# First attention of a four-stage network: transposes and value weighing one step later behind the scores, a third buffer for the first map, output weights in the raw weights' buffer

## The reference, cut to what matters

```python
qkv = hidden_states @ Wqkv_w.T + Wqkv_b
p1 = attn_map(q[:, :, :, 0], k[:, :, :, 0])      # causal softmax(q k / sqrt(128))
p2 = attn_map(q[:, :, :, 1], k[:, :, :, 1])
p = p1 - lam * p2
o = einsum('bhqk,bhke->bqhe', p, v)
o = o * rsqrt(mean(o * o) + EPS) * subln_w * (1 - LAMBDA_INIT)
return o.reshape(B, S, H * D) @ out_w.T + out_b
```

## Time and profile before

| | us |
|---|---|
| median of 3 runs | 1652.39 |
| the three runs | 1649.94 to 1653.19 |
| profiled execution | 1637.22 |
| its span | 1635.4 |

### The profile page before, as it was taken

The page is one execution under the profiler, slowest core; times in us unless marked ns, Lnnn a source line. Parts: engine busy times, 40 slices in busy tenths (PEclk is TensorE's granted clock), DMA queues, the critical chain, the costliest instruction groups (busy, mean ns, idle before and its releaser), DMA issues.

```text
span 1635.4 us, 30982 instructions
## 1 busy us (share of the span) xinstructions
PE 1526.0 (93%) x10518; PEld 1317.8 (81%) x10518; DVE 1105.6 (68%) x2963; ACT 938.1 (57%) x2054; POOL 637.2 (39%) x578
## 2 busy tenths in 40 slices
PE   8899999999999999999998999899999999998996
PEld 7888888888888677688987888888888886776885
DVE  7667767677745787574687676676767377884756
ACT  5666565665544577653656556556655346775453
POOL 2635444654561100243545445444654510031642
PEclk9999999999999999999999999999999999999998
DMA  3110000020120432124310100000202113322233
GB/s 133 46 53 17 27 1 16 26 90 3 40 70 10 71 56 52 30 108 142 110 73 14 65 17 27 17 4 22 92 1 57 52 32 63 59 65 81 68 133 111
DMA packets 48202, 88.08 MB, mean 54 GB/s; under 512 B 9600, under 2 KB 30480, under 8 KB 46928
## 3 DMA queue, kind: packets, MB, share of 16 engines
q1 hardware_dynamic: 43552, 75.28, 16.1%
q0 software_dynamic: 3744, 10.26, 1.8%
q10 hardware_dynamic: 768, 0.79, 0.2%
HBM read 60.18 MB, written 19.76 MB: 49 GB/s over the span
## 4 chain that ended last, share of the span: by engine, by line
PE 62%; DVE 15%; ACT 10%; issue 8%; POOL 4%; ACTq 1%; DMA 1%; DVEq 0%; POOLq 0%; SPq 0%
PE ps L410 15%; PE ps L412 14%; PE ps L411 14%; PE ps L1193 4%; PE ps L1210 4%; PE ps L1153 4%; ACT E L1407 4%; DVE E L1816 2%; PE ps L916 2%; POOL E L2286 2%; ACT PT_h L1389 1%; DVE On L1724 1%; PE ps L1189 1%; PE ps L846 1%; POOL xs L2397 1%
## 5 line engine op out<-in xcount | busy, mean ns | idle before, releaser
L1407 ACT ACTIVATE E<-E,nmax 128x128 f32<-128x128 f32 (+7 forms) x256 | 197.3, 772 | 211.6 <-DVE nmax L1816 211.1
L2283 POOL TENSOR_SCALAR E<-E,mixc 128x128 f32<-128x128 f32 (+7 forms) x128 | 97.6, 762 | 400.9 <-DVE mixc L1782 400.9
L1568 ACT ACTIVATE PT<-ps 128x512 f32<-128x512 f32 x288 | 154.9, 600 | 58.7 <-PE ps L1193 57.7
L2286 POOL TENSOR_TENSOR E<-E 128x128 f32<-128x128 f32 (+7 forms) x128 | 182.8, 1428 | 10.7
L410 PE MATMUL ps<-V_h,PT_h 128*128 128x256 f32 x576 | 164.7, 286 | 1.7 <-DVE O L1794 1.7
L412 PE MATMUL ps<-V_h,PT_l 128*128 128x256 f32 x576 | 162.7, 283 | 0.0
L411 PE MATMUL ps<-V_l,PT_h 128*128 128x256 f32 x576 | 162.7, 282 | 0.0
L410 PE MATMUL ps<-K_h,Q_h 128*128 128x512 f32 (+3 forms) x384 | 142.7, 372 | 6.3 <-DVE nmax L1816 2.9
L1789 DVE TENSOR_TENSOR PT_l<-ps,PT_h 128x128 fp32r<-128x128 f32 (+7 forms) x128 | 96.7, 755 | 63.2 <-ACT PT_h L1389 62.6
L2036 DVE CUSTOM_DVE_ANT_0 masked<-ps,causal 128x128 bf16<-128x128 f32 (+3 forms) x256 | 110.9, 487 | 39.7 <-PE ps L1153 38.0
L411 PE MATMUL ps<-K_l,Q_h 128*128 128x512 f32 (+3 forms) x384 | 133.8, 348 | 0.0
(11 more groups left out here) (267 smaller groups left out, 4579.1 us busy)
## 6 DMA issues: line engine op xcount, KB each, us to landing
Wa_raw<-in_wa SPq DMA_DIRECT2D x8, 1024.0 KB, 6.0
Fw_raw<-in_fa SPq DMA_DIRECT2D x32, 256.0 KB, 2.7
E_raw<-in_fe SPq DMA_DIRECT2D x8, 768.0 KB, 7.5
xs<-in_xs SPq DMA_DIRECT2D x2, 2967.0 KB, 12.0
Wo_raw<-in_wo SPq DMA_DIRECT2D x8, 512.0 KB, 3.6
yg<-ys SPq DMA_DIRECT2D x8, 512.0 KB, 5.7
xg<-xs SPq DMA_DIRECT2D x6, 645.0 KB, 7.8
KS<-QK_h SPq DMA_DIRECT2D x56, 64.0 KB
```

The costliest lines, as they stand in the source:

```text
L1407: nc.scalar.activation(e[:, 0:w], e[:, 0:w], ACT.Exp, scale=-1.0, bias=nmax[:, s % 4, m:m + 1], accum_out=lsum[:, s % 4, m:m + 1]).then_in ...
L1568: nc.scalar.activation(PT[:, at:at + HALF], bank1(RING1 + n % RING1), ACT.Exp, scale=SCALE1).then_inc(t_used, 1)
L2283: nc.gpsimd.tensor_scalar(e2, e2, mixc[:, n % 4:n % 4 + 1], 1.0, ALU.mult, ALU.mult).then_inc(mix_scaled, 1)
L2286: nc.gpsimd.tensor_tensor(e1, e1, e2, ALU.add).then_inc(p_ready, 1)
```

## The change

- The transposes of a map are issued three steps behind its scores, not two (`TURN_LAG`), and with them `high` and `low`. The weighing and `output` are issued four steps behind, not three (`WEIGH_LAG`); `squares` start at step 5, not 4.
- `E1` has three buffers, `E2` still two. VectorE's second maximum of step s, from step 2 on, also waits for `p_ready` of step s - 2.
- The tail begins with one more transpose ("t" 13) and one more weighing ("v" 12); in the groups with units the tokens are dealt out anew.
- `Wo_raw` is no buffer of its own; it is the first half of `Wa_raw`. So the load of the output weights waits until the next group's `Wa_raw` has been split (step 11), and the load of `Wa_raw` waits until the output weights of the group before have been subtracted (`wo_lo`).

```diff
+E1_RING = 3
+TURN_LAG, WEIGH_LAG = 3, 4
...
-        E1 = [sb(f"E1_{i}", [P, T], F32, s) for i in range(2)]
+        E1 = [sb(f"E1_{i}", [P, T], F32, s) for i in range(E1_RING)]
...
-        Wo_raw = sb("Wo_raw", [P, 4, HID], F32, s)
+        Wo_raw = Wa_raw[:, 0].rearrange("p (c n) -> p c n", n=HID)
...
         if last:
-            return [("t", STEPS0 - 2), ("r", 0), ("v", STEPS0 - 3), ("n", 0), ("n", 1), ("t", STEPS0 - 1), ("o", 0),
-                    ("v", STEPS0 - 2), ("o", 1), ("v", STEPS0 - 1)]
-        return [("t", STEPS0 - 2), *u[0:2], ("v", STEPS0 - 3), *u[2:4], ("t", STEPS0 - 1), ("v", STEPS0 - 2), ("r", 0),
-                *u[4:9], ("v", STEPS0 - 1), *u[9:10], ("r", 1), *u[10:]]
+            return [("t", STEPS0 - 3), ("v", STEPS0 - 4), ("t", STEPS0 - 2), ("r", 0), ("v", STEPS0 - 3), ("n", 0), ("n", 1),
+                    ("t", STEPS0 - 1), ("o", 0), ("v", STEPS0 - 2), ("o", 1), ("v", STEPS0 - 1)]
+        return [("t", STEPS0 - 3), *u[0:2], ("v", STEPS0 - 4), *u[2:4], ("t", STEPS0 - 2), ("v", STEPS0 - 3), ("r", 0),
+                *u[4:6], ("t", STEPS0 - 1), ("v", STEPS0 - 2), *u[6:9], ("v", STEPS0 - 1), *u[9:10], ("r", 1), *u[10:]]
...
         def next_wa(b, g):
             sp.wait_ge(wa_lo, 4 * (b * GROUPS0 + g) + 4)
+            sp.nop(nofuse=True)
+            sp.wait_ge(wo_lo, b * GROUPS0 + g + 1)
+            sp.nop(nofuse=True)
             load_wa(g + 1)
+
+        def load_wo(b, g):
+            sp.wait_ge(wa_lo, 4 * (b * GROUPS0 + g) + 8)
+            sp.nop(nofuse=True)
+            sp.dma_start(Wo_raw, d["wo0"][g]).then_inc(wo_in, 16)
...
             sp.wait_ge(pj_dve, it * UNITS_IT + UNITS_IT)
             sp.nop(nofuse=True)
-            sp.wait_ge(wo_lo, it + 1)
-            sp.dma_start(Wo_raw[:], d["wo0"][g]).then_inc(wo_in, 16)
             load_ba(g + 1)
...
+            load_wo(b, 0)
+            if b == 0:
                 sp.wait_ge(w2_ready, 4)
...
                 group_loads(b, g)
+                load_wo(b, g)
...
             for s in range(STEPS0):
-                if s >= 2:
-                    transpose_p(s - 2)
+                if s >= TURN_LAG:
+                    transpose_p(s - TURN_LAG)
...
-                if s >= 3:
-                    weigh_values(s - 3)
+                if s >= WEIGH_LAG:
+                    weigh_values(s - WEIGH_LAG)
...
-                if s >= 2:
-                    high(s - 2)
+                if s >= TURN_LAG:
+                    high(s - TURN_LAG)
...
-                if s >= 4:
-                    squares(s - 4)
+                if s > WEIGH_LAG:
+                    squares(s - WEIGH_LAG - 1)
...
-                if s >= 2:
-                    low(s - 2)
+                if s >= TURN_LAG:
+                    low(s - TURN_LAG)
...
-                for m, e in ((0, E1[s % 2]), (1, E2[s % 2])):
+                for m, e in ((0, E1[s % E1_RING]), (1, E2[s % 2])):
+                    if m == 1 and s >= 2:
+                        dve.wait_ge(p_ready, STEPS0 * it + s - 1)
                     dve.wait_ge(s_ready[m], STEPS0 * it + s + 1)
```

More of the change, by code:

```diff
@@ L915, in transpose_p @@
                 for kb in range(q_tile(n, last) + 1):
-                    mm = nc.tensor.transpose(ps[2][:, tile(kb)], E1[n % 2][:, tile(kb)], ident[:])
+                    mm = nc.tensor.transpose(ps[2][:, tile(kb)], E1[n % E1_RING][:, tile(kb)], ident[:])
                 mm.then_inc(pt_ps, 1)
             for s in range(STEPS0):
-                if s >= 2:
-                    transpose_p(s - 2)
+                if s >= TURN_LAG:
+                    transpose_p(s - TURN_LAG)
                 if s == 0:
@@ L1442, in attn0_group @@
                         act.wait_ge(wo_scaled, KC * it + KC)
[L1443 removed]
+                        nc.scalar.copy(Wo_h[:], Wo_raw).then_inc(wo_hi, 1)
                     squares(n - 1)
@@ L1806, in attn0_group @@
                     out_normalise(it - 1, g + 1, s - 2)
-                if s >= 2:
-                    low(s - 2)
+                if s >= TURN_LAG:
+                    low(s - TURN_LAG)
                 if s == NT:
                     project_out(s, 0)
-                    output(s - 3)
-                for m, e in ((0, E1[s % 2]), (1, E2[s % 2])):
+                    output(s - WEIGH_LAG)
+                for m, e in ((0, E1[s % E1_RING]), (1, E2[s % 2])):
+                    if m == 1 and s >= 2:
+                        dve.wait_ge(p_ready, STEPS0 * it + s - 1)
                     dve.wait_ge(s_ready[m], STEPS0 * it + s + 1)
@@ L2279, in attn0_group @@
                 w = (q_tile(n, last) + 1) * P
-                e1, e2 = E1[n % 2][:, 0:w], E2[n % 2][:, 0:w]
+                e1, e2 = E1[n % E1_RING][:, 0:w], E2[n % 2][:, 0:w]
                 pool.wait_ge(mix_ready, STEPS0 * it + n + 1)
@@ L2297, in attn0_group @@
             pool.wait_ge(wo_hi, it + 1)
-            low(Wo_l[:], Wo_raw[:], Wo_h[:]).then_inc(wo_lo, 1)
+            low(Wo_l[:], Wo_raw, Wo_h[:]).then_inc(wo_lo, 1)
         def ffn_split(b, c):
```

2 lines of the change are left out of this document (1 added, 1 removed).

## The result

The changed kernel took 1664.5 us (median of 4 runs, 1664.2 to 1667.6), the kernel before, timed beside it, 1652.3 (4 runs, 1649.9 to 1653.2). Ratio 1.0080, 95% interval 1.0063 to 1.0098: 12 to 13 us slower. The forecast was 1660, 7.6 over before, in a range of 1644 to 1668.

The account below looks back on a forecast made before the run. A gapless ring of ScalarE and VectorE bounds most steps, TensorE a middle group's steps 10 to 12 and its end. Middle +2.5, first -3.9, last groups +9.0 make +7.6 us; on the timed median 1652.4 that gives 1660, range 1644 to 1668.

Parts of the forecast that it names:

- Ring: Steps 2 to 9 of a middle group, paced by ScalarE and VectorE without a gap: narrower casts and subtractions, -1.95 us.
- Steps 10 to 12: Middle group, paced by TensorE: the widest map arrives here, +2.25 us, bounds 0 and +2.65.
- Steps 13 to 15 and tail: End of a middle group: steps -0.7 us; in the tail -1.45 for an earlier first unit, +2.5 for moved work.
- Middle groups together: Four groups: +0.6 us each, +2.5 for all four; bounds of one -1.6 and +1.5.
- First groups: First group of each batch row, two: ScalarE and VectorE pace steps 2 to 15; together -3.9 us, bounds -9 and 0.
- step 10's +1.7: First group, step 10: the widest cast and subtraction replace the narrowest, +1.7 us.
- Step 11's -1.0: First group, step 11: VectorE's 1.10 us wait for the weighing of map 7 goes, -1.0 us.
- step 9's -0.5: First group, step 9: map 6 is cast instead of waiting for map 7's transposes, -0.5 us.
- Last groups: Two groups, tail begins with eight-block map 13: +2.8 us for serial cast and subtraction, +1.7 for clock, 4.5 each.
- the upper bound of 8: Last groups, 8 us each if the scaling of the outputs also falls behind GpSimd's last subtraction.
- Edits at nothing: Third map buffer, second maximum's new wait, shared weight buffer and moved loads: claimed to take no time.
- Rival 1: TensorE's waits for GpSimd's sum were path time: -34.3 us, 1618; chance 5%.

Follow-up runs that it names:

- clock_fill: The changed kernel plus six unread matmuls before the first output transpose of step 8 in middle and last groups; 1664.3 us, ratio 1.0049 to before.
- cast_late: The changed kernel with ScalarE's cast of the output weights one weighing later in the last groups' tail; 1662.9 us, ratio 1.0036 to before.
- product_one: The changed kernel with two of three passes of the output products left out in steps 8 to 11, middle and last groups; 1646.2 us, one execution.
- lag_none: The changed kernel with lags two and three and the old tails in every group, all else kept; 1650.6 us, ratio 0.9994 to before.
- lag_last: lag_none, but with lags three and four and the new tail in the last group of each row; 1664.5 us, ratio 1.0078 to before.

## Why the prediction was right, and where its sizes were off

The direction, its reason and the place of the largest term held.

- **Ring.** Steps 4 to 7 shortened by 0.24, 0.64, 0.24, 0.24, as worked out. Steps 2 to 9 of the first middle group gave -1.4 of the -1.95. Step 3 lost 0.1 instead of gaining 0.13. The period into step 8 grew by 0.3, the cost of the fall of the clock (9.42 before, 9.75 in the changed kernel, 9.41 in clock_fill and in cast_late's group without a fall).
- **Steps 10 to 12.** +1.88, -1.52, +2.27 = +2.6 in the first middle group, +2.3 in the second row's (forecast 2.25). That TensorE sets them with the longer lags: shown by product_one against the changed kernel.
- **Steps 13 to 15 and tail.** -0.9 (-0.7) and +1.2 (+1.05).
- **Middle groups together.** +1.4 to +1.6 each against +0.6, 3.5 us more over four. The step that failed: I looked at what fills TensorE's idle places and not at what is laid bare. The wait for GpSimd's sum in step 8 had covered most of another, for the turned outputs' subtraction (0.8 before); without it TensorE idles 2.2 us there in one piece, and the clock falls, in this execution in all four groups. That is 0.3 to 0.5 a group; the other half is spread over the terms above. The upper bound of +1.5 was also summed wrongly: with +2.65 for steps 10 to 12 the terms give +1.05, and all four groups lie above that.
- **First groups.** Predicted -3.9 together, -3.7 in the profiles, but only about -2 without the falls of the clock that the profiled execution of before happened to have, so the agreement is luck. I took two such falls as the rule; lag_none has neither. In the first row step 10's +1.7 and the tail came as worked out (+1.7, and +1.1 for +0.95). Step 11's -1.0 and step 9's -0.5 did not: against before they measure -1.1 and -0.7, but against lag_none -0.24 each, the narrower map alone. What I took for VectorE's wait for a weighing, which the lag would remove, was the price of the fall.
- **Last groups.** Predicted 2.8 for the serial chain and 1.7 for the clock, 4.5 each; measured 7.0 and 4.3. The size of the chain is right: with the scalings freed, cast_late's last groups are 2.7 and 2.5 longer than before's. Missed as a likely term was the cast of the output weights, which stood at the weighing of map 13 and by the change came later in the tail (fifth token instead of third), where GpSimd's subtraction fell on all four scalings: 2.1. I had it only as the condition of the upper bound of 8. The fall of the clock costs 1.5 (tails of 39.1 against 37.6), 2.4 where it is twice as long; it came in seven of the eight tails of this form (changed, lag_last, clock_fill, product_one).
- **What was to be seen.** Waits for GpSimd gone: yes. Waits for the maximum over 20 us: no, 11.8; TensorE stood earlier in the step, at the output transposes and at L927. Middle groups of 106 to 107.5 us: no, 107.7 to 110.5; those of the second row had taken 108.4 and 109.1 already before, which this mark overlooked. Idle time of 3 us for the subtraction (L1800) in the last tail: 0.95 only, as the weighing of map 12 filled the rest; the 2.88 came behind it, at the output transposes. Map 14's transposes started at 422.43, not at 420.7: the tail began 0.9 later, and map 13's transposes and map 12's weighing themselves waited for VectorE (0.5 and 0.9).
- **Edits at nothing.** Shown by lag_none, within 0.1% by the medians (0.9984 to 1.0005).
- **The sum.** 1660 stood on the timed median plus 7.6, and the terms now measure 13.3 in the traces: middle groups 3.5 above the forecast, last groups 2.2 above, first groups level by luck.
- **Rival 1.** The waits were not path time: the buffer was added, the 34.3 us of waits went, and every middle group became longer. The Trainium skill's rule on a repeating gap ("Perfetto Trace Analysis", section "Identifying Performance Opportunities"), which says only that it can mean too few buffers, therefore did not hold in this case.

## What to carry to other kernels

Here the fullest engine's longest wait was worth nothing, because two other engines formed a closed ring; measure the distance between the ring's own instructions before counting a wait as time. A longer lag moves the widest piece of work later: look at which engine is full where it lands, and in a tail with nothing to fill, expect the whole serial chain. After reordering a tail, look again at what now runs beside what; here one cast moved by one weighing was worth 2 to 4.5 us a row, and combined with the longer lag only where it pays it made the faster kernel.

## What the runs showed of the hardware

- VectorE's scalings of 128x256 between SBUF tiles take 0.35 us each alone. In the tail of the changed kernel the first of them, started together with GpSimd's subtraction of 128x1024 (2.34 us), lasted until that ended: 3.23 for four against 1.14 in cast_late.
- A fall of TensorE's clock has no fixed price: 17 matmuls for 30 in a step cost 0.3 to 0.5 us where another pair of engines sets the pace, about 1.3 in a first group (97.4 and 96.0 at the same order), 1.5 to 2.4 in a tail where TensorE is the path. Nor is it certain behind the same idle time: it came behind 11 of 16 waits of 2.2 us in step 8, and behind one of the two waits of 2.88 us in the changed kernel.
- The routed experts' stretch took 75 or 85 us for the same instructions, from one occasion to the next. So the spans of kernels profiled on different occasions could not be subtracted here.
